# Keys and values of the recurrence stage as three fp32r products of high and low parts, with one context buffer

## The reference

```python
x = x + mamba(_layernorm(x))                       # state-space block, d_inner 1024, 16 states
x = x + cross_attention(_layernorm(x), ctx_512)    # 16 heads of 32; keys and values from ctx_512
x = x + moe(_layernorm(x))                         # 4 experts, top 2

# in mamba, for each time step t:
dA = exp(A * dt_t[..., None])
h = h * dA + (x_t * dt_t)[..., None] * B_t[:, None, :]
y = einsum('bdn,bn->bd', h, C_t)
# in cross_attention:
kh = ctx @ Wk + bk          # 750 x 256 by 256 x 512, for each of 8 batches
vh = ctx @ Wv + bv
```

## Time and profile before

| | |
|---|---|
| runs | 2930.95, 2944.82, 2938.28 us; median 2938.28 |
| profiled execution | 2944.2 us, of which the span of instructions 2942.5 |
| TensorE clock granted, mean | 0.915 |
| busy share of the span | PE 85%, DVE 49%, ACT 41%, POOL 44% |
| first and last scan of the recurrence | begin at 382.5 and 1064.9 us |
| DVE scans, 256 | 527.6 us busy, mean 2080 ns |

### The profile page before, as it was taken

The page is one execution under the profiler, slowest core; times in us unless marked ns, Lnnn a source line. Parts: engine busy times, 40 slices in busy tenths (PEclk is TensorE's granted clock), DMA queues, the critical chain, the costliest instruction groups (busy, mean ns, idle before and its releaser), DMA issues. The chain is left out here.

```text
span 2942.5 us, 39312 instructions
## 1 busy us (share of the span) xinstructions
PE 2491.5 (85%) x14320; PEld 2017.7 (69%) x14320; DVE 1430.8 (49%) x1880; ACT 1206.3 (41%) x2611; POOL 1297.2 (44%) x892
## 2 busy tenths in 40 slices
PE   5998569999999974788988988883589989999991
PEld 4984358888888862555665665652478888888881
DVE  5342479999999961455554454443021212121213
ACT  2333367777777621333433333332233333333330
POOL 3321247777777740544544544542563090009004
PEclk9998779999999997799989999886799999999996
DMA  9323765555565445434434452415531031002015
GB/s 290 126 105 95 222 192 170 164 160 157 175 172 175 133 137 133 114 93 104 113 95 94 106 119 70 108 29 187 179 107 57 29 122 42 15 29 79 29 64 157
DMA packets 257561, 349.20 MB, mean 119 GB/s; under 512 B 36574, under 2 KB 183966, under 8 KB 256270
## 3 DMA queue, kind: packets, MB, share of 16 engines
q1 hardware_dynamic: 235790, 281.32, 34.5%
q0 software_dynamic: 16256, 55.85, 5.7%
q10 hardware_dynamic: 5376, 10.23, 0.9%
HBM read 215.97 MB, written 131.35 MB: 118 GB/s over the span
## 5 line engine op out<-in xcount | busy, mean ns | idle before, releaser
L655 POOL TENSOR_TENSOR s_hc<-s_h,s_Cc 128x896 f32<-128x896 f32 x256 | 494.9, 1938 | 206.7 <-DVE s_h L760 102.4
L760 DVE TENSOR_TENSOR_SCAN s_h<-s_decay,s_ub 128x928 f32<-128x928 f32 x256 | 527.6, 2080 | 11.1 <-ACT s_decay L690 2.7
L798 PE MATMUL s_yps<-s_hc,s_ident 128*128 128x224 f32 x2048 | 431.1, 354 | 1.1 <-POOL s_hc L655 1.1
L1016 POOL TENSOR_TENSOR t_part<-t_pT 125x672 f32<-125x672 f32 x128 | 206.0, 1609 | 437.4 <-ACT t_pT L1159 437.0
L690 ACT ACTIVATE s_decay<-s_dt,s_A 128x224 f32<-128x224 f32 x1024 | 388.0, 470 | 18.4 <-DVE s_h L760 18.3
L1698 DVE TENSOR_TENSOR e_hl<-e_ps,e_hh 128x256 fp32r<-128x256 f32 x256 | 108.7, 425 | 573.0 <-ACT e_ps L1744 573.0
L798 PEld LDWEIGHTS s_yps<-s_hc,s_ident 128*128 128x128 f32 x2048 | 369.3, 191 | 2.0 <-POOL s_hc L655 1.4
L1046 DVE TENSOR_REDUCE t_nmax<-t_ps 112x1 f32<-112x752 f32 x256 | 239.8, 937 | 184.7 <-PE t_ps L1227 184.3
L1770 PE MATMUL e_ps<-e_xTh,e_w1h 128*128 128x256 f32 x1024 | 293.3, 286 | 23.5 <-DVE e_xTl L1690 23.5
L1159 ACT ACTIVATE t_pT<-t_ps 125x448 f32<-125x448 f32 x384 | 181.2, 545 | 317.8 <-PE t_ps L1251 306.5
L1743 ACT ACTIVATE e_hh<-e_ps,e_b 128x256 fp32r<-128x256 f32 x256 | 121.8, 476 | 421.9 <-PE e_ps L1772 421.7
(11 more groups left out here) (202 smaller groups left out, 4375.1 us busy)
## 6 DMA issues: line engine op xcount, KB each, us to landing
s_ut<-ut_d SPq DMA_DIRECT2D x192, 128.0 KB, 3.3
e_stage<-in_L_ffn_We POOLq DMA_DIRECT2D x24, 1024.0 KB, 5.6
t_k<-kh_d SPq DMA_DIRECT2D x64, 375.0 KB, 6.5
xs_d<-a_zero POOLq DMA_DIRECT2D x30, 512.0 KB, 12.5
s_Cc<-cs_d SPq DMA_DIRECT2D x8, 1792.0 KB, 9.6
kh_d<-s_kh SPq DMA_DIRECT2D x32, 375.0 KB, 2.7
kl_d<-s_kl SPq DMA_DIRECT2D x32, 375.0 KB, 2.8
v_d<-s_v SPq DMA_DIRECT2D x48, 250.0 KB
```

The lines of the kernel that those rows point to most:

```text
L655: nc.gpsimd.tensor_tensor(hc[:, u % 2, k], h[:, u % 2, k, :, 2:SLOT], Cc[:, b % 2, k], ALU.mult).then_inc(hc_done, 1)
L760: nc.vector.tensor_tensor_scan(h[:, u % 2, k].rearrange("p n t -> p (n t)"), decay[:, u % 2, k].rearrange("p n t -> p (n t)"), ub[:, s % 2 ...
L798: ins = nc.tensor.matmul(yps[:, u % 2, 0:L], ident[:], hc[:, u % 2, :, n], start=(n == 0), stop=(n == NS - 1))
L1016: nc.gpsimd.tensor_tensor(part[:], p[:, 0:3], p[:, 3:6], ALU.add).then_inc(sum_step, 1)
```

## The change

What it does:

1. Keys and values are each a sum of three fp32r products (high x high, high x low, low x high) in place of one float32 product: 12 matmuls of 376 columns for a key unit (pieces of 3, 3 and 6), 6 of 512 columns for a value tile. The two halves of the keys are 376 wide and overlap by two columns.
2. `Wk` and `Wv` are loaded into the second half of `s_hc`; ACT makes their high parts and POOL the low parts, once, at the stage's start. ACT does this, and the high part of context 0, ahead of `decays(0)`.
3. There is one context (`cxh`, `cxl`). It is loaded as `raw`, which is the memory of the keys `s_keys` (before `s_kh`, `s_kl`). So the load of context b+1 waits until all keys of batch b are stored, and is moved in SP's loop from c = 2 to c = 7, behind the stores of unit 6's keys. ACT makes the high part (`high_context`) after `keys_values(u-2)` and ahead of `decays(u)` for u = 8, 16, ...; POOL makes the low part after unit u-1; PE waits for it at the batch's first keys.
4. `V_TILES` gives two value tiles to units 1, 3 and 5 and none to unit 7. A key store is two DMAs in place of one.

```diff
-        wk, wv, bkc = sb("wk", [P, CK, DM]), sb("wv", [P, CK, DM]), sb("bkc", [P, KC])
-        cxT = sb("cxT", [P, 2, CK, CTX])
-        kh, kl = sb("kh", [P, CTX], F32R), sb("kl", [P, CTX], F32R)
+        wkh, wkl, wvh, wvl = (sb(n, [P, CK, DM], F32R) for n in ("wkh", "wkl", "wvh", "wvl"))
+        cxh, cxl = sb("cxh", [P, CK, CTX], F32R), sb("cxl", [P, CK, CTX], F32R)
+        keys = sb("keys", [P, 2, 2 * EVEN])
+        kh, kl = (keys[:, i].bitcast(F32R) for i in range(2))
+        raw = keys[:].rearrange("p i t -> p (i t)")[:, 0:CK * CTX].rearrange("p (k t) -> p k t", k=CK)
...
-        V_TILES = [(0, 1), (2, 3), (4,), (5,)]
+        V_TILES = [(0, 1), (2, 3), (4, 5), ()]
...
             def load_ctx(b):
-                if b >= 2:
-                    sp.wait_ge(v_mm, NC * (b - 1))
-                sp.dma_start(cxT[:, b % 2], ctxT_in[b].rearrange("(k p) t -> p k t", p=P)).then_inc(ctx_loaded[b % 2], 16)
+                if b >= 1:
+                    sp.wait_ge(kh_stored, 32 * KC * b)
+                    sp.wait_ge(kl_stored, 32 * KC * b)
+                sp.dma_start(raw, ctxT_in[b].rearrange("(k p) t -> p k t", p=P)).then_inc(ctx_loaded, 16)
...
-                if c == 2 and b + 1 < B:
-                    load_ctx(b + 1)
                 if u >= 1 and u <= UNITS:
                     store_keys_values(u - 1)
+                if c == CC - 1 and b + 1 < B:
+                    load_ctx(b + 1)
...
+            def low_context(b):
+                pool.wait_ge(ctx_high, b + 1)
+                nc.gpsimd.tensor_tensor(cxl[:], raw, cxh[:].bitcast(F32), ALU.subtract).then_inc(ctx_split, 1)
+            for i, (high, low, w) in enumerate(((wkh, wkl, wk_raw), (wvh, wvl, wv_raw))):
+                pool.wait_ge(w_high, i + 1)
+                nc.gpsimd.tensor_tensor(low[:], w, high[:].bitcast(F32), ALU.subtract).then_inc(w_split, 1)
+            low_context(0)
...
+                if u % CC == CC - 1 and b + 1 < B:
+                    low_context(b + 1)
...
+            def high_context(b):
+                act.wait_ge(ctx_loaded, 16 * (b + 1))
+                act.wait_ge(k_mm, KC * b)
+                act.wait_ge(v_mm, NC * b)
+                nc.scalar.activation(cxh[:], raw, ACT.Copy).then_inc(ctx_high, 1)
...
+            act.wait_ge(consts, 16 * 5)
+            for high, w in ((wkh, wk_raw), (wvh, wv_raw)):
+                nc.scalar.activation(high[:], w, ACT.Copy).then_inc(w_high, 1)
+            high_context(0)
             for u in range(UNITS + 1):
                 if u >= 2:
                     keys_values(u - 2)
+                if u % CC == 0 and 0 < u < UNITS:
+                    high_context(u // CC)
                 if u < UNITS:
                     decays(u)
...
+            def product(out, high, low, n, first, last):
+                (sh, mh), (sl, ml) = high, low
+                return nc.tensor.matmul(out, (sh, sh, sl)[n], (mh, ml, mh)[n], start=first and n == 0, stop=last and n == 2)
...
-                    pe.wait_ge(ctx_loaded[b % 2], 16 * (b // 2 + 1))
+                    pe.wait_ge(ctx_split, b + 1)
...
-            pe.wait_ge(consts, 16 * 5)
+            pe.wait_ge(w_split, 2)
```

More of the change, by code:

```diff
@@ L484, in state_space @@
     HIGH, LOW = 0, 1
+    EVEN = HALF + 1
     with ctx:
@@ L515, in state_space @@
             sem(n) for n in ("consts", "mask_loaded", "a_loaded", "a_step", "a_done", "diag_zeroed", "edge_zeroed"))
-        bt_loaded, c_loaded, ctx_loaded = ([sem(f"{n}{i}") for i in range(2)] for n in ("bt_loaded", "c_loaded", "ctx_loaded"))
+        bt_loaded, c_loaded = ([sem(f"{n}{i}") for i in range(2)] for n in ("bt_loaded", "c_loaded"))
+        ctx_loaded, ctx_high, ctx_split, w_high, w_split = (
+            sem(n) for n in ("ctx_loaded", "ctx_high", "ctx_split", "w_high", "w_split"))
         ut_loaded, dt_loaded, late_loaded = ([sem(f"{n}{i}") for i in range(2)] for n in ("ut_loaded", "dt_loaded", "late_loaded"))
@@ L523, in state_space @@
             sem(n) for n in ("k_mm", "v_mm", "k_done", "k_split", "v_done", "kh_stored", "kl_stored"))
-        V_TILES = [(0, 1), (2, 3), (4,), (5,)]
+        wk_raw, wv_raw = (hc[:, 1].rearrange("p s n t -> p (s n t)")[:, i * CK * DM:(i + 1) * CK * DM].rearrange("p (k n) -> p k n", k=CK)
+                          for i in range(2))
+        V_TILES = [(0, 1), (2, 3), (4, 5), ()]
         block = ctx.enter_context(nc.Block())
@@ L587, in store, with store_half @@
                 sp.dma_start(cols(y_d, u), y[:, u % 2]).then_inc(y_stored[u % 2], 16)
+            def store_half(out, t, done):
+                sp.dma_start(out[:, 0:EVEN], t[:, 0:EVEN]).then_inc(done, 16)
+                sp.dma_start(out[:, EVEN:CTX], t[:, EVEN + 2:2 * EVEN]).then_inc(done, 16)
             def store_keys_values(u):
@@ L592, in store_keys_values @@
                     sp.wait_ge(k_done, KC * b + q + 1)
-                    sp.dma_start(kh_d[b, q], kh[:].bitcast(F32)).then_inc(kh_stored, 16)
+                    store_half(kh_d[b, q], keys[:, 0], kh_stored)
                     sp.wait_ge(k_split, KC * b + q + 1)
-                    sp.dma_start(kl_d[b, q], kl[:].bitcast(F32)).then_inc(kl_stored, 16)
+                    store_half(kl_d[b, q], keys[:, 1], kl_stored)
                 else:
@@ L638, in _ @@
                 sp.wait_ge(s, 16 * UNITS // 2)
-            sp.wait_ge(kh_stored, 16 * B * KC)
-            sp.wait_ge(kl_stored, 16 * B * KC)
+            sp.wait_ge(kh_stored, 32 * B * KC)
+            sp.wait_ge(kl_stored, 32 * B * KC)
             for s in v_stored:
@@ L663, in _ @@
             act.wait_ge(a_done, 1)
+            def high_context(b):
[3 more added lines that the diff above has]
+                nc.scalar.activation(cxh[:], raw, ACT.Copy).then_inc(ctx_high, 1)
             def keys_values(u):
                 b, q = u // CC, u % CC // 2
-                if u == 0:
-                    act.wait_ge(consts, 16 * 5)
                 if u % 2 == 0:
                     act.wait_ge(k_mm, KC * b + q + 1)
+                    if q == 0:
+                        act.wait_ge(ctx_split, b + 1)
                     if KC * b + q >= 1:
-                        act.wait_ge(kh_stored, 16 * (KC * b + q))
+                        act.wait_ge(kh_stored, 32 * (KC * b + q))
                         act.wait_ge(k_split, KC * b + q)
-                    nc.scalar.activation(kh[:].rearrange("p (a c) -> p a c", a=2), kvps[:, :, 0:HALF], ACT.Identity,
+                    nc.scalar.activation(kh.rearrange("p (a c) -> p a c", a=2), kvps[:, :, 0:EVEN], ACT.Identity,
                                          bias=bkc[:, q:q + 1]).then_inc(k_done, 1)
@@ L732, in low_keys @@
                 if KC * b + q >= 1:
-                    dve.wait_ge(kl_stored, 16 * (KC * b + q))
-                nc.vector.scalar_tensor_tensor(out=kl[:].rearrange("p (a c) -> p a c", a=2), in0=kvps[:, :, 0:HALF],
-                                               scalar=bkc[:, q:q + 1], in1=kh[:].bitcast(F32).rearrange("p (a c) -> p a c", a=2),
+                    dve.wait_ge(kl_stored, 32 * (KC * b + q))
+                nc.vector.scalar_tensor_tensor(out=kl.rearrange("p (a c) -> p a c", a=2), in0=kvps[:, :, 0:EVEN],
+                                               scalar=bkc[:, q:q + 1], in1=kh.bitcast(F32).rearrange("p (a c) -> p a c", a=2),
                                                op0=ALU.add, op1=ALU.subtract).then_inc(k_split, 1)
@@ L804, in keys_values @@
                 if u % CC == 0 and pieces[0] == 0:
-                    pe.wait_ge(ctx_loaded[b % 2], 16 * (b // 2 + 1))
+                    pe.wait_ge(ctx_split, b + 1)
                 if u % 2 == 0:
                     if pieces[0] == 0 and u >= 1:
-                        pe.wait_ge(v_done, NC * b + V_TILES[q][0])
+                        pe.wait_ge(v_done, NC * b + (V_TILES[q][0] if V_TILES[q] else NC))
                     for i in pieces:
[L810 to L813, removed]
+                        a, k, n = i // 6, i // 3 % 2, i % 3
+                        cols = slice(a * (CTX - EVEN), a * (CTX - EVEN) + EVEN)
+                        ins = product(kvps[:, a, 0:EVEN], (wkh[:, k, q * P:(q + 1) * P], cxh[:, k, cols]),
+                                      (wkl[:, k, q * P:(q + 1) * P], cxl[:, k, cols]), n, k == 0, k == CK - 1)
+                    if pieces[-1] == 11:
                         ins.then_inc(k_mm, 1)
@@ L818, in keys_values @@
                     for i in pieces:
[L819 to L823, removed]
+                        if i // 6 < len(V_TILES[q]):
+                            t, k, n = V_TILES[q][i // 6], i // 3 % 2, i % 3
+                            cols = slice(t * CT, (t + 1) * CT)
+                            ins = product(kvps[0:CT, t % 2], (cxh[:, k, cols], wvh[:, k]), (cxl[:, k, cols], wvl[:, k]), n, k == 0, k == CK - 1)
+                            if i % 6 == 5:
                                 ins.then_inc(v_mm, 1)
@@ L835, in _ @@
                     if k >= 1:
```

(2 more changed lines are left out.)

5 lines of the change are left out of this document (3 added, 2 removed).

## The result

| | before | after |
|---|---|---|
| median of 4 runs | 2937.73 us | 2997.61 us (2988.83 to 2998.48) |
| ratio of the runs | | 1.0197, 95% interval 1.0166 to 1.0228 |
| profiled execution (span) | 2944.2 (2942.5) | 2998.5 (2996.8) |
| granted clock, mean | 0.915 | 0.903 |
| last scan of the recurrence begins | 1064.9 | 1120.4 |

What follows compares the result with a forecast made beforehand. DVE was taken as the pace, 81.6 us a batch, held up a little by PE through the keys. Terms -15 + 51 + 13 + 13 = +62 us on the median 2938.3 made 3000, eight times in ten between 2979 and 3022.

Steps and rivals of the forecast that it cites:

- seven stalls for the decays: Between batches, DVE stands still 7.3 us at 7 places, waiting for ACT's decays: 51 us, bounds 40 to 66.
- PE's half clock behind them: After each batch-end stall, PE resumes at half the granted clock: 13 us in all, bounds 0 and 24.
- the start: ACT's first decays wait for constants and copies: unit 1 begins 11.0 later, plus 2 for PE's clock; 13, bounds 9 and 18.
- fewer waits for keys and fills: Shorter PE products inside the batches cut DVE's waits: 15 us less over the stage, bounds 10 and 22.
- a sign of being wrong: DVE's units inside a batch not at 81.6 us a batch would mean that PE is still the pace.
- The chain: At batch ends, low-key store, context load, ACT's copy and decays run in series; DVE scans at T + 17.8, before T + 10.5.
- the 1.8 a place: Time put on PE's half clock at each of seven batch ends; slack in the first segments takes about 0.7.
- rival B: PE stays behind after each stall, first keys late: gain about 5, clock cost 24, 3021 us; chance 0.19.
- The DMA's constant part: For the batch-end context load: about 2.0 us per transfer whatever its size, plus 1.8 for the bytes, 3.8 us.
- the 0.2 a pair: Wait that may stay in pairs of units with two value tiles: 20.6 us of PE against 20.4 of DVE.
- A (the clock stays up): After the batch-end stalls the clock stays up, or PE's slack swallows its fall: 2985 us; chance 0.15.
- C (not slower): The chain across batches hides in unit 15 through quick transfers: 2932 us at the limit; chance 0.03.

Runs made afterwards that it cites:

- e7: The kernel before with half of its key and value products left out; 2968.1 us, ratio 1.0098 to the kernel before.
- e1: The changed kernel with ACT's copy of the next context put behind the new batch's first decays; 2942.2 us, ratio 1.0005 to the kernel before.
- e4: The changed kernel with 26 unused products on PE ahead of the first fill of each batch but the first; 2986.2 us, ratio 1.0137 to the kernel before.
- e2: The changed kernel with each context load after the first issued twice, one after the other; 3035.5 us, ratio 1.0300 to the kernel before.

## Why the prediction was right

The forecast was 3000 us, the measured median is 2997.6, and it came about by the mechanism forecast. Its terms, for the stage (measured: the stalls from DVE's waits, the rest from the unit lengths):

| term | forecast | measured |
|---|---|---|
| seven stalls for the decays | 51 | 46.4 |
| PE's half clock behind them | 13 | 15 |
| the start | 13 | 9.7 at unit 1 |
| fewer waits for keys and fills | -15 | -15 |
| sum | 62 | 56 (last scan's end: 55.5) |

- *What bounds it.* DVE's 81.6 us a batch as the floor is shown by e7, at 81.7. The batch before was 84.4, where the prediction added up 83.9. But inside the changed kernel a batch is not at the floor, which the prediction had named as a sign of being wrong: without its stall it is 91.4 - 6.7 = 84.7. Of the 3.0 above the floor 2.1 are the half clock's, and 0.8 are the 0.27 in each of units 3, 5 and 7, where PE still makes the keys a little late.
- *The chain.* Each link was nearly right: the store landed in 2.1 us, not 2.5; the load in 4.2, not 4.3; the copy of 1500 elements took 1.45, not 1.48. The low keys came 0.3 later than taken, half of it a wait of 0.15 for the high keys. DVE scans at T + 17.4 in place of 17.8, and unit 15 itself is 0.3 longer, so the stall is 6.6 and not 7.3. That the order on ACT alone exposes the chain, e1 shows.
- *The clock.* The fall after a long idle time came at all seven places, as the rule of the Trainium skill ("TensorE: Matmul & The Clock Gate", section "HAM oscillation — how this bites in real kernels") would have it, and e4 prices it at 15. The size was right, but what it is made of was partly luck: the 1.8 a place were put on the fills of the first segments, and the late first keys stood only in the bound of 24 and in rival B. Measured, unit 0 is 0.8 longer and unit 1, by its late low keys (1.28 us at 596.11), 1.4.
- *The DMA's constant part*, by the Trainium skill ("DMA: Bandwidth & Descriptors", section "Anatomy of one DMA"), gave 3.8 us for the load; the seven loads of the changed kernel landed after 4.0 to 4.5, so the row-based value of 4.3 was the better one. That section gives its figures for DMAs which GpSimd issues, and this load is issued by SyncE, so it is no test of them.
- *The gain.* In the stalled kernel it is about 15: a batch without its stall (17.55 - 10.83 = 6.7) and without the clock (2.1) is 82.6 against 84.4, which is 1.8 for each of seven batches, and units 1 to 7 of the first are 1.7 shorter. But it is only so large because PE catches up in each stall. With the stalls gone (e1) a batch is 83.4, so the change's own gain is 1.0 a batch, 8 in all. The step "at most 2.3 us a batch can be had" was right as a bound, and the 0.2 a pair that I left for PE was in truth 0.27 for each of three units. In e1 another 0.9 stand behind the wait for POOL's low part, which has a price only once the stall is gone.
- *The start* was 3 too dear at unit 1: PE's half clock there took nothing in unit 0, where no sums stand. It lasted to 416.2, though, and units 1 and 2 took 10.19 and 10.91 us, against 9.92 and 9.79 in e4, where it ended 2.0 us after unit 1 began and not 6.0. By that comparison 1.4 us of it came later; in the table they are taken off the gain.
- *Rivals.* A (the clock stays up): refuted, all seven fell. B (PE stays behind): its condition came true, the first keys are late, but PE had caught up by unit 2, so the clock cost 15 and not 24, and the gain was 15 and not 5. C (not slower): the seven stalls exclude it. (The terms' lowest bounds add up to 2965, not to the 2967 stated; nothing hangs on it.)

What the whole runs add: attention, which the change doesn't touch, took 928.6 us in the profiled execution before, 926.0 after and 937.7 when the changed kernel ran again. That moves a whole run by 10 us, so that 2997.6 lay 2 from 3000 while the stage's sum was 6.5 too high is partly luck.

## What to carry to other kernels

Where an engine executes in order, look at what stands behind a new waiting instruction before looking at the wait: here a store of 2.1 us, a load of 4.2 and a copy of 1.4, at seven places, made the kernel slower because the decays, DVE's input, stood behind them, and exchanging two instructions on ACT gave 56 us back. A buffer shared to save memory turns a prefetch into a chain of store, load and use; that is affordable only if nobody in the chain feeds the bound. And a stage's gain from relieving an engine is capped by the next engine's own program, which its timeline gives before any experiment.

## What the runs showed of the hardware

- At all 14 places of the changed kernel's two executions where PE was idle for 6.2 to 7.0 us between batches, the granted clock fell to 0.50 within the idle time, 2.3 to 4.9 us after it began, and stood there for 6.8 or 10.2 us, until 3.1 to 6.4 us after PE had resumed. With e4's filling, an idle time of 3.0 us at one place was followed by 3.4 us at 0.50, from 1.4 us after PE had resumed. The other six, filled, stayed at 1.00.
- An untouched stage differed by up to 22 us from one execution to another: attention took 921.6 us in e1 and 943.2 in e2. Terms of some us are to be read from the stage that a change is in.
- Leaving out work whose result steers later work (e7) changed the experts' time by 44 us, more than the effect sought.
- GpSimd's subtraction of 1500 elements took 3.35 us, and ScalarE's copy of as many 1.45.

```profile
L695 ACT ACTIVATE s_cxh<-s_keys x8: 1437/1455/1457, 393.5 to 1031.4; 128x1500 fp32r<-128x1500 f32 x8
L665 POOL TENSOR_TENSOR s_cxl<-s_keys,s_cxh x8: 3342/3348/3359, 397.3 to 1034.2; 128x1500 fp32r<-128x1500 f32 x8
```
